# One graph layer on one core: user groups of 512 columns and a last one of 272, in place of 20 groups of 500

## What is computed

```python
h = item_feat @ W_item.T + b_item          # items x 128
b = x @ W_user.T + b_user                  # users x 128
x = _layernorm(x + jax.nn.relu(adj @ h + b), axis=-1)
```

## Time and profile before

| | us |
|---|---|
| median of 3 runs | 1142.09 |
| lowest and highest run | 1141.98, 1143.6 |
| span of the profiled execution | 1140.9 |
| TensorE matmuls busy | 1121.9 (98%) |
| VectorE busy | 942.8 (83%) |
| ScalarE busy | 805.8 (71%) |
| mean rate of the transfers | 365 GB/s |

### The profile page before, as it was taken

How to read it: one execution, slowest core, us unless ns; L and a number is a source line. 1 busy time by engine, 2 the same in 40 slices (tenths; PEclk the granted TensorE clock), 3 DMA queues, 4 the chain that set the end, 5 groups by cost and what they waited for, 6 DMA issues and landing times. The chain is left out here.

```text
span 1140.9 us, 14807 instructions
## 1 busy us (share of the span) xinstructions
PE 1121.9 (98%) x5038; PEld 931.9 (82%) x5038; DVE 942.8 (83%) x684; ACT 805.8 (71%) x583; POOL 34.0 (3%) x27
## 2 busy tenths in 40 slices
PE   6999999999999999999999999999999999999997
PEld 5888888888888888888888888888888888888885
DVE  4889888888888888888888887888888888888884
ACT  5677767677767777776777777767777777676764
POOL 3440000000000000000000000000000000000000
PEclk8999999999999999999999999999999999999999
DMA  8999999999999999999999999999999999999992
GB/s 297 352 367 402 391 378 368 375 375 378 371 367 382 373 369 379 369 372 374 367 382 365 370 365 392 359 392 362 379 362 387 369 374 368 387 364 366 383 374 78
DMA packets 67471, 415.91 MB, mean 365 GB/s; under 512 B 7872, under 2 KB 11264, under 8 KB 67456
## 3 DMA queue, kind: packets, MB, share of 16 engines
q1 hardware_dynamic: 67456, 415.71, 95.6%
HBM read 410.44 MB, written 5.24 MB: 364 GB/s over the span
## 5 line engine op out<-in xcount | busy, mean ns | idle before, releaser
L403 DVE TENSOR_TENSOR adj_lo<-adj,adj_hi 128x2000 fp32r<-128x2000 f32 (+1 forms) x400 | 873.0, 2191 | 131.1 <-ACT adj_hi L301 130.9
L301 ACT CAST adj_hi<-adj 128x2000 fp32r<-128x2000 f32 (+1 forms) x400 | 730.7, 1827 | 294.3 <-PE acc L246 262.0
L242 PE MATMUL acc<-adj_hi,h_hi 128*128 128x500 f32 x1600 | 630.0, 394 | 0.2 <-POOL h_lo L367 0.2
L243 PE MATMUL acc<-adj_hi,h_lo 128*128 128x500 f32 x1600 | 622.4, 389 | 0.0
L246 PE MATMUL acc<-adj_lo,h_hi 128*128 128x500 f32 x1600 | 429.1, 388 | 0.0
L242 PEld LDWEIGHTS acc<-adj_hi,h_hi 128*128 128x128 f32 x1600 | 301.4, 188 | 63.0 <-POOL h_lo L367 0.5
L246 PEld LDWEIGHTS acc<-adj_lo,h_hi 128*128 128x128 f32 x1600 | 301.1, 188 | 62.1
L243 PEld LDWEIGHTS acc<-adj_hi,h_lo 128*128 128x128 f32 x1600 | 301.9, 189 | 60.6
L418 DVE BATCH_NORM_STATS2 stats<-z_ps 128x6 f32<-128x128 f32 x80 | 17.8, 285 | 32.1 <-PE z_ps L256 32.1
L227 PE MATMUL h_ps<-w_item,items 128*128 128x128 f32 (+1 forms) x158 | 23.3, 296 | 11.1 <-DMA bias_user<-b_user 6.6
L367 POOL TENSOR_TENSOR h_lo<-h_full,h_hi 128x512 fp32r<-128x512 f32 (+1 forms) x20 | 32.8, 1643 | 43.3 <-ACT h_hi L342 43.3
(11 more groups left out here) (19 smaller groups left out, 37.0 us busy)
## 6 DMA issues: line engine op xcount, KB each, us to landing
adj<-adj_t SPq DMA_DIRECT2D x380, 1000.0 KB, 7.3
adj<-adj_t SPq DMA_DIRECT2D x20, 500.0 KB, 5.5
out<-normed SPq DMA_DIRECT2D x20, 256.0 KB, 7.6
xg<-x_t SPq DMA_DIRECT2D x20, 250.0 KB, 4.4
items<-item_t SPq DMA_DIRECT2D x19, 256.0 KB, 4.7
adj<-adj_tail SPq DMA_DIRECT2D x20, 31.2 KB, 4.8
items<-item_t SPq DMA_DIRECT2D x1, 136.0 KB, 4.5
w_item<-w_item_t SPq DMA_DIRECT2D x1, 64.0 KB, 1.8
```

The costliest lines, as they stand in the source:

```text
L242: nc.tensor.matmul(into, h_hi[:, k, :], adj_hi[:, s, c, :], start=(k == 0), stop=False)
L243: nc.tensor.matmul(into, h_lo[:, k, :], adj_hi[:, s, c, :], start=False, stop=False)
L301: nc.scalar.copy(adj_hi[:, s, start:, :], adj[:, a, start:, :]).then_inc(hi_made, 1)
L403: nc.vector.tensor_tensor(adj_lo[:, s, start:, :], adj[:, a, start:, :], adj_hi[:, s, start:, :].bitcast(F32), ALU.subtract).then_inc(lo_m ...
```

## The change

The groups have 512 columns, 19 of them, and the last one has the remaining 272 (`WIDE`, `NARROW`, `width`). There are still 20 groups. Buffers get 512 columns, every operation on them takes `0:u` with the group's width, the rows of a load get 8192 bytes (4352 in the last group), and the last group has input arrays of its own. Since the last group differs, the loops run over groups 2 to 17 in eight rounds, and groups 18 and 19 are written out on every engine. The core of the diff; the same replacements stand in `load_x`, `relu`, the last tile's small casts and subtracts, and in the loops of the other engines:

```diff
-GROUP = 500
-GROUPS = N_USER // GROUP
+WIDE = 512
+NARROW = N_USER % WIDE
+GROUPS = N_USER // WIDE + 1
 BLOCKS = 4
-BLOCK = GROUP // BLOCKS
...
-PAIRS = GROUPS // 2
+LOOP_PAIRS = (GROUPS - 4) // 2
...
+def width(g):
+
+    return NARROW if isinstance(g, int) and g == GROUPS - 1 else WIDE
...
-        adj = sb("adj", [P, ADJ_RING, PER_TILE, GROUP])
-        adj_hi = sb("adj_hi", [P, PART_RING, PER_TILE, GROUP], F32R)
-        adj_lo = sb("adj_lo", [P, PART_RING, PER_TILE, GROUP], F32R)
-        xg = sb("xg", [P, GROUP])
+        adj = sb("adj", [P, ADJ_RING, PER_TILE, WIDE])
+        adj_hi = sb("adj_hi", [P, PART_RING, PER_TILE, WIDE], F32R)
+        adj_lo = sb("adj_lo", [P, PART_RING, PER_TILE, WIDE], F32R)
+        xg = sb("xg", [P, WIDE])
...
+                u = width(g)
+                tail_rows = adj_tail[g] if u == WIDE else tail_narrow
+                full_rows = adj_t[g] if u == WIDE else adj_narrow
...
-                sp.dma_start(adj[:, t % ADJ_RING, PER_TILE - n:PER_TILE, :],
-                             adj_t[g, :, t * PER_TILE:t * PER_TILE + n, :]).then_inc(adj_landed[t % ADJ_RING], 16)
+                sp.dma_start(adj[:, t % ADJ_RING, PER_TILE - n:PER_TILE, 0:u],
+                             full_rows[:, t * PER_TILE:t * PER_TILE + n, :]).then_inc(adj_landed[t % ADJ_RING], 16)
...
-                into = acc[parity][:, 0:GROUP]
+                u = width(g)
+                into = acc[parity][:, 0:u]
...
-                        nc.tensor.matmul(into, h_hi[:, k, :], adj_hi[:, s, c, :], start=(k == 0), stop=False)
-                        nc.tensor.matmul(into, h_lo[:, k, :], adj_hi[:, s, c, :], start=False, stop=False)
+                        nc.tensor.matmul(into, h_hi[:, k, :], adj_hi[:, s, c, 0:u], start=(k == 0), stop=False)
+                        nc.tensor.matmul(into, h_lo[:, k, :], adj_hi[:, s, c, 0:u], start=False, stop=False)
...
-            with pe.Fori(1, PAIRS) as i:
+            with pe.Fori(1, LOOP_PAIRS + 1) as i:
                 group(2 * i, 0)
                 group(2 * i + 1, 1)
+            group(GROUPS - 2, 0)
+            group(GROUPS - 1, 1)
             turn_back(GROUPS - 1)
...
-                nc.scalar.copy(adj_hi[:, s, start:, :], adj[:, a, start:, :]).then_inc(hi_made, 1)
+                nc.scalar.copy(adj_hi[:, s, start:, 0:u], adj[:, a, start:, 0:u]).then_inc(hi_made, 1)
...
-                nc.vector.tensor_tensor(adj_lo[:, s, start:, :], adj[:, a, start:, :],
-                                        adj_hi[:, s, start:, :].bitcast(F32), ALU.subtract).then_inc(lo_made, 1)
+                nc.vector.tensor_tensor(adj_lo[:, s, start:, 0:u], adj[:, a, start:, 0:u],
+                                        adj_hi[:, s, start:, 0:u].bitcast(F32), ALU.subtract).then_inc(lo_made, 1)
...
-                nc.vector.tensor_tensor(z_t[:, :, 0:BLOCK],
-                                        relu_t[:, :].rearrange("p (b n) -> p b n", b=BLOCKS),
-                                        xg[:, :].rearrange("p (b n) -> p b n", b=BLOCKS),
+                u = width(g)
+                nc.vector.tensor_tensor(z_t[:, :, 0:u // BLOCKS],
+                                        relu_t[:, 0:u].rearrange("p (b n) -> p b n", b=BLOCKS),
+                                        xg[:, 0:u].rearrange("p (b n) -> p b n", b=BLOCKS),
                                         ALU.add).then_inc(z_added, 1)
...
-        "adj_t": np.ascontiguousarray(groups[:, :, :full].reshape(GROUPS, GROUP, FULL, P).transpose(0, 3, 2, 1)),
+        "adj_t": np.ascontiguousarray(groups[:, :, :full].reshape(GROUPS - 1, WIDE, FULL, P).transpose(0, 3, 2, 1)),
...
+        "adj_narrow": np.ascontiguousarray(adj[wide:, :full].reshape(NARROW, FULL, P).transpose(2, 1, 0)),
+        "tail_narrow": np.ascontiguousarray(adj[wide:, full:].T),
+        "x_narrow": np.ascontiguousarray(x[wide:].T),
```

More of the change, by code:

```diff
@@ L91, in chunk, with gnn_kernel @@
     return {AT_TAIL: FULL, AT_USER: FULL + 1}.get(c, t * PER_TILE + c - AT_FULL)
-def gnn_kernel(nc, adj_t, adj_tail, x_t, item_t, w_item_t, b_item, w_user_t, b_user, out):
+def gnn_kernel(nc, adj_t, adj_tail, x_t, adj_narrow, tail_narrow, x_narrow, item_t, w_item_t, b_item, w_user_t, b_user, out):
     with ExitStack() as ctx:
@@ L118, in gnn_kernel @@
         ident = sb("ident", [P, P])
-        relu_t = sb("relu_t", [P, GROUP])
+        relu_t = sb("relu_t", [P, WIDE])
         z_t = sb("z_t", [P, BLOCKS, P])
@@ L210, in _ @@
             load_group(1)
-            with sp.Fori(1, PAIRS) as i:
+            with sp.Fori(1, LOOP_PAIRS + 1) as i:
                 load_group(2 * i)
                 load_group(2 * i + 1)
+            load_group(GROUPS - 2)
+            load_group(GROUPS - 1)
             store(GROUPS - 2)
@@ L306, in relu @@
                     act.wait_ge(z_added, g)
-                nc.scalar.activation(relu_t[:, :], acc[parity][:, 0:GROUP], ACT.Relu,
+                u = width(g)
+                nc.scalar.activation(relu_t[:, 0:u], acc[parity][:, 0:u], ACT.Relu,
                                      bias=bias_user[:, 0:1]).then_inc(relu_done, 1)
@@ L344, in _ @@
             group(1, 1)
-            with act.Fori(1, PAIRS) as i:
+            with act.Fori(1, LOOP_PAIRS + 1) as i:
                 group(2 * i, 0)
                 group(2 * i + 1, 1)
+            group(GROUPS - 2, 0)
+            group(GROUPS - 1, 1)
             relu(GROUPS - 1, 1)
@@ L395, in split_lo @@
                     dve.wait_ge(hi_made, steps_to(g, t) - 1)
[L396 to L399, removed]
+                    nc.vector.tensor_tensor(adj_lo[:, s, AT_TAIL, 0:u], adj[:, a, AT_TAIL, 0:u],
+                                            adj_hi[:, s, AT_TAIL, 0:u].bitcast(F32), ALU.subtract)
+                    nc.vector.tensor_tensor(adj_lo[:, s, AT_USER, 0:u], xg[:, 0:u],
+                                            adj_hi[:, s, AT_USER, 0:u].bitcast(F32),
                                             ALU.subtract).then_inc(lo_made, 1)
@@ L463, in _ @@
             group(1)
-            with dve.Fori(1, PAIRS) as i:
+            with dve.Fori(1, LOOP_PAIRS + 1) as i:
                 group(2 * i)
                 group(2 * i + 1)
+            group(GROUPS - 2)
+            group(GROUPS - 1)
             add_x(GROUPS - 1)
@@ L479 @@
     full = FULL * P
-    groups = np.asarray(adj).reshape(GROUPS, GROUP, N_ITEM)
+    wide = N_USER - NARROW
+    adj, x = np.asarray(adj), np.asarray(x)
+    groups = adj[:wide].reshape(GROUPS - 1, WIDE, N_ITEM)
     arrays = {
-        "adj_t": np.ascontiguousarray(groups[:, :, :full].reshape(GROUPS, GROUP, FULL, P).transpose(0, 3, 2, 1)),
+        "adj_t": np.ascontiguousarray(groups[:, :, :full].reshape(GROUPS - 1, WIDE, FULL, P).transpose(0, 3, 2, 1)),
         "adj_tail": np.ascontiguousarray(groups[:, :, full:].transpose(0, 2, 1)),
-        "x_t": np.ascontiguousarray(np.asarray(x).reshape(GROUPS, GROUP, HID).transpose(0, 2, 1)),
+        "x_t": np.ascontiguousarray(x[:wide].reshape(GROUPS - 1, WIDE, HID).transpose(0, 2, 1)),
+        "adj_narrow": np.ascontiguousarray(adj[wide:, :full].reshape(NARROW, FULL, P).transpose(2, 1, 0)),
+        "tail_narrow": np.ascontiguousarray(adj[wide:, full:].T),
+        "x_narrow": np.ascontiguousarray(x[wide:].T),
         "item_t": np.ascontiguousarray(np.asarray(L0_gnn_item_feat).T),
@@ L497 @@
     got = r.results[0]["out"]
-    return np.ascontiguousarray(got[:, :BLOCK].transpose(0, 2, 1, 3).reshape(N_USER, HID))
+    return np.concatenate([got[:-1].transpose(0, 2, 1, 3).reshape(wide, HID),
+                           got[-1, :NARROW // BLOCKS].transpose(1, 0, 2).reshape(NARROW, HID)])
```

11 lines of the change are left out of this document (6 added, 5 removed).

## The result

The changed kernel takes 1116.65 us (median of 4 runs, 1116.21 to 1117.07) against 1142.55 before: 0.9744 of it, 95% interval 0.9705 to 0.9784. Rival (c), the step, put it at 1119, 2.4 us above what was measured.

The account below looks back on a forecast made before the run. TensorE's matmul stream was taken as the bound. Stream 0, feeders 0, start +0.15, end -0.43 and loop 0 summed to -0.28 us, giving 1141.8 us against a median of 1142.09, range 1138 to 1151.

Parts of the forecast that it names:

- Rival (c): TensorE's stream: a 500-column matmul already pays for 512, so -22.8 us, 1119 us; chance 0.09.
- the price of 12 more columns: Wide matmuls in TensorE's stream: +0.0050 us each if the extra is fixed, +22.8 us, cancelled by the narrow ones.
- the other 0.019 us: Warm 500-column matmul: 0.2273 us less 0.2083 for its columns; taken as a fixed cost or going with the columns.
- straight line: TensorE's stream: matmul price linear in columns, so wide and narrow matmuls cancel to 0, the mean staying 500 columns.
- The second term: Narrow matmuls of the last group: 0.1323 us each with a fixed extra, 240 x -0.0950 = -22.8 us.
- rival (a): Last group's stream: a floor under the narrow matmul, spacing held by the weight load; 1155 us at 0.188; chance 0.12.
- The cold rows: Matmuls at 1.2 GHz before the warm stream: 0.41 us for 500 columns, one column a cycle; taken as against a step.
- The feeders: VectorE, ScalarE and loads in the narrow group: each under TensorE's time, 0 us, at most 1 to 3 us of stalls.
- rival (b): Last group starved by a code fetch or VectorE falling behind: 1 to 5 us, 1143 to 1147 us; chance 0.09.
- Rival (d): Loads become the bound if new addresses cost bandwidth: 373 GB/s needed against 423, 11 us per percent beyond 12%; chance 0.04.
- The start: Chain before the first matmul: longer load, cast and subtract, +0.15 us, bounds 0 and +0.4.
- The end: Relu and sum with x behind the last matmul, each 228 columns shorter: -0.43 us together.

Follow-up runs that it names:

- wide_pitch516: The changed kernel with rows of adj_hi and adj_lo 516 columns apart instead of 512: 1142.5 us, ratio 0.999.
- wide_w32: The changed kernel with an unused pad of 32 bytes ahead of the weights h_hi and h_lo: 1153.19 us, ratio 1.005.
- first probe: TensorE alone, 25 blocks of 48 matmuls differing in columns, row distance or type; 512 float32r columns with rows 516 apart took 0.2310 us a matmul.
- aligned500: The kernel before with 500-column matmuls, rows 512 columns apart, and two pads putting split parts and weights on multiples of 256 bytes: 1139.59 us, ratio 0.9956.
- stream512_al: The kernel before with groups of 500 users, 512 columns streamed (12 zeros), and two pads putting split parts and weights on multiples of 256 bytes: 1143.42 us.
- pitch512: The kernel before with rows of adj_hi and adj_lo 512 columns apart, 500 of them used: 1144.11 us, ratio 1.0005.
- third probe: TensorE alone, 39 blocks of 36 float32r matmuls, shifting moving rows and weights and varying length; 512 columns, both shifted by 64 bytes: 0.2275 us.
- the second: Probe with blocks of 40 matmuls, moving rows or weights shifted by some bytes; moving rows 256 bytes on: 0.2273 us, weights 32 bytes on: 0.2333.

## Why the prediction was wrong

What bounds the kernel was right: TensorE's stream before and after, all feeders behind it.

The step that failed is the price of 12 more columns. The prediction put the other 0.019 us of the warm matmul, beyond one column a cycle, on a straight line, fixed or in proportion to the columns, and so summed the stream to 0. 4560 wide matmuls should have cost 0.2323 us and cost 0.2269: -0.0054 x 4560 = -24.6 us. The runs show how the 0.019 us divide. 32 columns' time, 0.0133, is what 256 and 512 columns pay over their columns' time in the probes. The other 0.0056 is what a 500-column matmul pays beyond that in the kernels and a 512-column one does not, if weights and moving rows lie a multiple of 256 bytes apart. Off that distance a 512-column matmul pays up to 0.0064, and the straight line is nearly right: wide_pitch516 has 0.2317 where the forecast had 0.2323, and the fastest runs of wide_w32 take 1146 us. That wide_pitch516's median of 1142.5 us meets the forecast is luck, since it lies between its two clusters. So the gain needs both: 512 columns off the distance bring little or none of it (1137 us at best in wide_pitch516, 1146 in wide_w32, where before has 1142), and 500 columns at the distance only 3 us. The change got the distance by the way, because 512 x 4 bytes is a multiple of 256; neither the change nor the prediction aimed at it. The lengths between 256 and 512 lie on no line either: over their columns' time 384 columns pay 0.0140 us and 480 pay 0.0167 (first probe).

The second term is small: the narrow matmul, 0.125 for 0.132, 240 x -0.007 = -1.7 us. The floor of rival (a) does not exist. 1140.6 - 24.6 - 1.7 + 0.3 for the start = 1114.6, the span is 1115.0.

Rival (c) had the right effect (the 500-column matmul pays for 512 already: 0.2267 and 0.2268 in aligned500 and stream512_al) and the right size, -22.8 us; its chance of 0.09 was too low. Of its two causes, rows that straddle lines are worth 3 us (pitch512), and granules of columns fit only in part, since 504 columns off the distance cost 1.4 ns more than 500. That the weights' distance decides it stood nowhere, so that its 1119 us came in part by luck. The prediction counted the 0.019 us without explanation as a weak sign for it and the cold rows as a strong one against. They are no sign: in the rows of wide_w32 above, whose addresses are bad, a 512-column matmul at half clock takes 0.42 us (94.14 to 94.56), and 512 columns at 1.2 GHz are 0.427, and the changed kernel, with good addresses, starts three in 19.18 - 17.90 = 1.28 us of its timeline, 0.427 each, so that in these rows the cost shows only at the upper clock. The cold rows could speak neither for a step at the warm level nor against it.

The feeders: forecast 1.29 and 1.10 us for narrow tiles, measured 1.288 and 1.105; the group was not starved, rival (b) did not come. The 5 to 7 us for which TensorE stands in group 0 of three other kernels end with GpSimd's subtract, for which the code waits there, and are no sign of a fetch of code. Rival (d): the transfers reached 385 GB/s in the wide groups, above the 373 needed before; the new pitch of 39 x 4096 bytes shows no cost that reaches TensorE, as the Trainium skill ("DMA: Bandwidth & Descriptors", Latency and other measured facts) lets one expect of a pitch that is not such a power of two. The start: forecast +0.15, measured +0.46 (17.31 for 16.85), a little past the bound, most of it before the first cast (11.90 for 11.53). With one execution of each it speaks neither for nor against what the Trainium skill ("DMA: Bandwidth & Descriptors", How a descriptor splits into AXI transactions) gave for it, a load that costs nothing more. The end: forecast -0.43, measured -0.45.

What is not settled: why 500 columns at the same good distance take 0.2233 us in the first and third probe, 0.2270 in the second and 0.2267 in aligned500, what in the engine makes the distance count, and why shifts of 16 bytes don't follow it. Nor was it tried why GpSimd's last subtract takes 9 to 11 us in some executions.

## What to carry to other kernels

A float32r stream of 512-column matmuls at the upper clock has a price that depends on how far the moving rows lie from the weights, modulo 256 bytes (at 272 columns the probe shows none, 0.125 us either way): make both the row distance of the moving operand and the lengths of all buffers between it and the weights multiples of 256 bytes, and look at the spacing of the matmuls, not at their number. When the spacing in the trace is longer than columns over clock, and the rest has no explanation, the rest is the uncertain term. Measure it by length and by address in a kernel with matmuls alone before it is extended in a straight line. Padding is no neutral edit: 32 unused bytes cost 29 us here.

## What was not expected of the hardware

- 512-column float32r matmuls at the upper clock: 0.2269 us with weights and moving rows a multiple of 256 bytes apart, otherwise mostly 0.2333 (0.2290 to 0.2340 by the distance at shifts of 32 bytes and more). The Trainium skill ("TensorE: Matmul & The Clock Gate", Step-by-step: what each phase is for) has two independent read ports for the two, and loads of weights that take nothing from the moving operand. The runs don't show full independence for this type: the price depends on the two addresses together.
- Over their columns' time 256 and 512 float32r columns pay 13 ns (32 columns), 480 to 504 at the same distance up to 17. In bfloat16 512 columns took 0.2160 us, 2.7 ns over 512 / 2.4 GHz; there the trace agrees with the Trainium skill ("TensorE: Matmul & The Clock Gate", Back-to-back issue gap), which has N / 2.4 + 2.5 ns, and in float32r it does not.
- GpSimd's subtract of 128 x 384 numbers, 1.8 to 2.0 us in nine profiled executions, took 8.5 to 11.3 us in three, beside VectorE's subtracts. TensorE stood still for 5 to 7 us and ran on at half clock.
